# Packing attention's 74-row tail products by row copies, and holding GpSimd's residual addition

## The reference

```
x = x + relu(softmax(where(adj > 0, leaky_relu(h@a1 + (h@a2).T), -9e15)) @ h)   with h = layernorm(x) @ W
x = x + moe(layernorm(x))
```

## Time and profile before

| what | value |
|---|---|
| median of three runs | 265.56 us (265.4 to 267.12) |
| the profiled execution | 263.48 us |
| its span, first to last instruction | 261.7 us |
| TensorE busy | 250.5 us (96%) |
| VectorE, ScalarE, GpSimd busy | 180.9, 128.6, 90.1 us |
| granted TensorE clock, mean | 0.998 of full speed |

### The profile page before, as it was taken

How to read it: one execution, slowest core, us unless ns; L and a number is a source line. 1 busy time by engine, 2 the same in 40 slices (tenths; PEclk the granted TensorE clock), 3 DMA queues, 4 the chain that set the end, 5 groups by cost and what they waited for, 6 DMA issues and landing times.

```text
span 261.7 us, 4579 instructions
## 1 busy us (share of the span) xinstructions
PE 250.5 (96%) x1649; PEld 210.8 (81%) x1649; DVE 180.9 (69%) x429; ACT 128.6 (49%) x263; POOL 90.1 (34%) x113
## 2 busy tenths in 40 slices
PE   6799989999999999999999999999999999999990
PEld 1489989988888778778778889899977968879780
DVE  3988768996978977785762573847296685856931
ACT  2737786853765475555553121342447155454330
POOL 4334891000341432112120224118253834841502
PEclk9999999999999999999999999999999999999999
DMA  6990000320488888421211213136978679888001
GB/s 189 375 318 32 1 5 0 106 81 27 159 210 284 273 262 248 168 79 40 80 42 41 82 39 96 52 117 176 353 237 294 247 258 290 283 293 285 12 7 44
DMA packets 19210, 40.47 MB, mean 155 GB/s; under 512 B 2810, under 2 KB 3130, under 8 KB 19188
## 3 DMA queue, kind: packets, MB, share of 16 engines
q1 hardware_dynamic: 16196, 34.17, 39.5%
q0 software_dynamic: 2176, 4.80, 6.1%
q10 hardware_dynamic: 816, 1.21, 1.5%
HBM read 32.93 MB, written 8.31 MB: 158 GB/s over the span
## 4 chain that ended last, share of the span: by engine, by line
PE 87%; POOL 3%; DVE 2%; DMA 2%; issue 2%; ACT 2%; POOLq 1%; ACTq 0%
PE bank L1426 30%; PE bank L1690 12%; PE bank L1728 7%; PE bank L1364 6%; PE bank L1412 5%; PE bank L1756 5%; PE bank L1441 3%; PE bank L1660 2%; PE bank L1346 2%; DMA w_raw<-in_L_gnn_W_dram 2%; PE bank L1676 2%; PE bank L1703 2%; PE bank L1453 2%; PE bank L1464 2%; PE bank L1560 1%
## 5 line engine op out<-in xcount | busy, mean ns | idle before, releaser
L1426 PE MATMUL bank<-h_hi,pt_lo 128*128 128x512 f32 (+1 forms) x110 | 45.9, 417 | 0.0
L1426 PE MATMUL bank<-h_lo,pt_hi 128*128 128x512 f32 (+1 forms) x110 | 43.6, 396 | 0.0
L1426 PE MATMUL bank<-h_hi,pt_hi 128*128 128x512 f32 (+1 forms) x110 | 43.4, 394 | 0.0
L411 POOL TENSOR_TENSOR x_all<-x_all,w_raw 128x512 f32<-128x512 f32 x10 | 18.1, 1810 | 65.2 <-ACT w_raw L589 65.2
L1690 PE MATMUL bank<-prob,w 128*128 128x168 f32 x224 | 33.2, 306 | 0.0
L1690 PEld LDWEIGHTS bank<-prob,w 128*128 128x128 f32 x224 | 32.6, 189 | 0.7 <-issue 0.2
L754 ACT ACTIVATE adj_s<-bank,b_cols 128x168 f32<-128x168 f32 x28 | 11.3, 402 | 33.6 <-PE bank L1690 33.6
L1426 PEld LDWEIGHTS bank<-h_hi,pt_hi 128*128 128x128 f32 (+1 forms) x110 | 20.7, 188 | 4.9
L1426 PEld LDWEIGHTS bank<-h_hi,pt_lo 128*128 128x128 f32 (+1 forms) x110 | 20.7, 188 | 3.8
L1426 PEld LDWEIGHTS bank<-h_lo,pt_hi 128*128 128x128 f32 (+1 forms) x110 | 20.8, 189 | 3.6
L611 ACT ACTIVATE wide<-adj_s,off_b 128x1354 f32<-128x1354 f32 (+1 forms) x11 | 15.8, 1432 | 14.1 <-DVE off_b L887 14.1
(11 more groups left out here) (203 smaller groups left out, 558.1 us busy)
## 6 DMA issues: line engine op xcount, KB each, us to landing
w<-in_L_ffn_W_dram SPq DMA_DIRECT2D x16, 1024.0 KB, 6.7
adj_s<-in_adj_dram SPq DMA_DIRECT2D x10, 677.0 KB, 5.3
x_rows<-x_all SPq DMA_DIRECT2D x10, 257.0 KB, 3.2
out_dram<-x_all SPq DMA_DIRECT2D x10, 256.0 KB
...
```

What stands on the lines that cost most here:

```text
L411: pool.tensor_tensor(x_all[0:R, t, 0:D], x_all[0:R, t, 0:D], relu_s[0:R, :], ALU.add).then_inc(s_x1, 1)
L1426: ins = pe.matmul(o_ps[par][0:R, :], p[0:K, par, k, 0:R], h[0:K, k, :], start=(k == 0 and n == 0), stop=(k == NT - 1 and n == 2))
```

## The change

The last 74 columns of each row tile of probabilities are split as 64 (A) and 10 (B). The exponential of the 10 is written twice more behind the row, so that the last transposed tile has 94 rows: A, B, B, B. Three products A and three products B are then made by two: one of 128 rows with (low A, high A) against (high h of A, low h of A), and one of 94 rows with (high A, low B, high B, high B) against (high A, high B, low B, high B) of h. To have h in that order the last tile's transposed x is written with the same copies (`x_high`, `x_low` in two pieces), so that h(10) has 94 rows; ScalarE writes high h of A to `h_lo` too, VectorE writes low h of A to its lower half, and replaces the middle copy in `h_hi` by the low part with the help of a 0/1 column `is_lo`, which GpSimd makes in `low_rows`. Per row tile there are a second, short exponential, another copy in `p_high` and a third piece in `p_low`. GpSimd's `residual(t)` for t < 9 waits in addition until `p_low(t + 1)` of batch 2 is done, which in VectorE's order stands just ahead of the argument. Some small tiles of the last stage move into a tile that is free by then; this adds no instruction.

```diff
@@ -43,6 +43,10 @@
     TAIL = N - (NT - 1) * P
     CAP = N // E - 1
     S = (P, CAP - P)
+    TA = P // 2
+    TB = TAIL - TA
+    TD = TA + 3 * TB
+    NP = N + 2 * TB
     ROW = D + 2
     NOWHERE = 5000
     BATCH = ((0, 8), (8, NT - 1), (NT - 1, NT))
...
@@ -81,7 +85,7 @@
         adj_s = sb("adj_s", [P, 3, N], I32)
         wide = sb("wide", [P, 2, N])
         score2, f2b = wide[:, 0, :], wide[:, 1, :]
-        prob = sb("prob", [P, 2, N])
+        prob = sb("prob", [P, 2, NP])
         pt_hi = sb("pt_hi", [P, 2, NT, P], F32R)
         pt_lo = sb("pt_lo", [P, 2, NT, P], F32R)
         w12 = sb("w12", [P, 4, KC, D])
...
@@ -134,6 +139,7 @@
         pos = sb("pos", [P, NT])
 
         relu_s = w_raw[:, 0, 0:D]
+        h_pick = w_raw[:, 2, 0:D]
         xn2 = (w_raw[:, 2, 0:D], w_raw[:, 3, 0:D], adj_s[:, 0, 0:D].bitcast(F32))
         xg0 = adj_s[:, 2, 0:2 * D].bitcast(F32).rearrange("p (j n) -> p j n", j=2)
         b_rows = w_raw[0:E * KC, 1, 0:2 * P].rearrange("q (j p) -> q j p", j=2)
...
@@ -159,14 +165,12 @@
                                                                     ].rearrange("p (c n) -> p c n", c=KC)
                            for i in range(2)] for v in (h_hi, h_lo))
         b2_b = [prob[:, i, KC * CAP:KC * CAP + D] for i in range(2)] + [adj_s[:, 1, KC * CAP:KC * CAP + D].bitcast(F32)]
-        gate_s = sb("gate_s", [P, 2, E])
+        gate_s, emp = first[:, 0:2, :], first[:, 2:4, :]
+        dest, src = first[:, 4:6, :].bitcast(U32), first[:, 6:8, :].bitcast(U32)
         scale_s = sb("scale_s", [P, 2, 2])
         src0 = sb("src0", [P, 2], U32)
         sums = below[:, 0:6, :].rearrange("p t e -> p (t e)").rearrange("p (j e k) -> p j e k", j=2, k=3)
         gate0 = sb("gate0", [P, 2])
-        emp = sb("emp", [P, 2, E])
-        dest = sb("dest", [P, 2, E], U32)
-        src = sb("src", [P, 2, E], U32)
 
         banks = [ctx.enter_context(nc.psum_tensor(f"bank{i}", [P, 512], F32)) for i in range(8)]
         xt_ps = (banks[0], banks[1])
...
@@ -396,8 +399,22 @@
                 after(pool, s_f2, n, 2)
                 pool.tensor_tensor(dot[0:R, n % 2, :], xn[0:R, t, :], wa2_b[0:R, :], ALU.mult).then_inc(s_dot, 1)
 
+            def low_rows():
+
+
+                pool.memset(is_lo[:, 0:1], 1.0).then_inc(s_const, 1)
+                pool.wait_ge(s_const, 11)
+                pool.affine_select(out=is_lo[:, 0:1], in_=is_lo[:, 0:1], compare_op=ALU.is_ge, fill=0.0,
+                                   base=-(TA + TB), pattern=[[0, 1]], channel_multiplier=1).then_inc(s_const, 1)
+                pool.wait_ge(s_const, 12)
+                pool.affine_select(out=is_lo[:, 0:1], in_=is_lo[:, 0:1], compare_op=ALU.is_ge, fill=0.0,
+                                   base=TA + 2 * TB - 1, pattern=[[0, 1]], channel_multiplier=-1).then_inc(s_const, 1)
+                pool.wait_ge(s_const, 13)
+                pool.tensor_scalar(is_lo[:, 1:2], is_lo[:, 0:1], -2.0, 1.0, ALU.mult, ALU.add).then_inc(s_const, 1)
+
             for t in range(NT - 2):
                 power(t)
+            low_rows()
             f2_product(FCOL)
             f2_product(FCOL + 1)
             for t in range(NT - 2, NT):
...
@@ -408,6 +425,8 @@
             def residual(t):
                 R = rows(t)
                 pool.wait_ge(s_relu, t + 1)
+                if t < NT - 2:
+                    pool.wait_ge(s_plo[2], t + 2)
                 pool.tensor_tensor(x_all[0:R, t, 0:D], x_all[0:R, t, 0:D], relu_s[0:R, :], ALU.add).then_inc(s_x1, 1)
 
             def power2(t):
...
@@ -496,12 +515,20 @@
                 else:
                     if t >= 4:
                         act.wait_ge(s_h, t - 1)
-                    act.activation(xt_hi[:, par, :, 0:R], src_[:, :, 0:R], ACT.Copy).then_inc(s_xhi, 1)
+                    if t == NT - 1:
+                        act.activation(xt_hi[:, par, :, 0:TA], src_[:, :, 0:TA], ACT.Copy)
+                        act.activation(xt_hi[:, par, :, TA:TD].rearrange("p c (r n) -> p c r n", r=3),
+                                       src_[:, :, TA:TAIL].unsqueeze(2).broadcast_to([P, KC, 3, TB]), ACT.Copy
+                                       ).then_inc(s_xhi, 1)
+                    else:
+                        act.activation(xt_hi[:, par, :, 0:R], src_[:, :, 0:R], ACT.Copy).then_inc(s_xhi, 1)
 
             def h_high(t):
-                R, par = rows(t), t % 2
+                R, par = (rows(t) if t < NT - 1 else TD), t % 2
                 act.wait_ge(s_h, t + 1)
                 for j in range(2):
+                    if t == NT - 1:
+                        act.activation(h_lo[0:TA, t, j * H0:(j + 1) * H0], h_ps[par][j][0:TA, 0:H0], ACT.Copy)
                     ins = act.activation(h_hi[0:R, t, j * H0:(j + 1) * H0], h_ps[par][j][0:R, 0:H0], ACT.Copy)
                 ins.then_inc(s_hhi, 1)
 
...
@@ -600,7 +627,8 @@
                     act.activation(pt_hi[:, par, k0:k1, 0:R], v[:, :, 0:R], ACT.Copy).then_inc(s_phi[b], 1)
                 else:
                     act.activation(pt_hi[:, par, k0:k1 - 1, 0:R], v[:, 0:k1 - k0 - 1, 0:R], ACT.Copy)
-                    act.activation(pt_hi[0:TAIL, par, k1 - 1, 0:R], v[0:TAIL, k1 - k0 - 1, 0:R], ACT.Copy
+                    act.activation(pt_hi[0:TD, par, k1 - 1, 0:R], v[0:TD, k1 - k0 - 1, 0:R], ACT.Copy)
+                    act.activation(pt_lo[TA:P, par, k1 - 1, 0:R], v[0:TA, k1 - k0 - 1, 0:R], ACT.Copy
                                    ).then_inc(s_phi[b], 1)
 
             def low_slope(t):
...
@@ -617,7 +645,9 @@
 
                 after(act, s_pt[2], t, 2)
                 after(act, s_rinv, t, 2)
-                act.activation(prob[0:R, par, :], arg[t % 3][0:R, :], ACT.Exp,
+                act.activation(prob[0:R, par, N:NP].rearrange("p (r n) -> p r n", r=2),
+                               arg[t % 3][0:R, N - TB:N].unsqueeze(1).broadcast_to([R, 2, TB]), ACT.Exp)
+                act.activation(prob[0:R, par, 0:N], arg[t % 3][0:R, :], ACT.Exp,
                                accum_out=rsum[0:R, par, :]).then_inc(s_prob, 1)
 
             def x2_copy(t, par):
...
@@ -797,15 +827,36 @@
                 if t >= 4:
                     dve.wait_ge(s_h, t - 1)
                 v = xt_ps[par][:, :].rearrange("p (c n) -> p c n", c=KC)
+                if t == NT - 1:
+                    dve.tensor_tensor(xt_lo[:, par, :, 0:TA], v[:, :, 0:TA], xt_hi[:, par, :, 0:TA].bitcast(F32),
+                                      ALU.subtract)
+                    dve.tensor_tensor(xt_lo[:, par, :, TA:TD].rearrange("p c (r n) -> p c r n", r=3),
+                                      v[:, :, TA:TAIL].unsqueeze(2).broadcast_to([P, KC, 3, TB]),
+                                      xt_hi[:, par, :, TA:TD].rearrange("p c (r n) -> p c r n", r=3).bitcast(F32),
+                                      ALU.subtract).then_inc(s_xlo, 1)
+                    return
                 dve.tensor_tensor(xt_lo[:, par, :, 0:R], v[:, :, 0:R], xt_hi[:, par, :, 0:R].bitcast(F32),
                                   ALU.subtract).then_inc(s_xlo, 1)
 
             def h_low(t):
                 R, par = rows(t), t % 2
                 dve.wait_ge(s_hhi, t + 1)
+                if t == NT - 1:
+                    dve.wait_ge(s_const, 14)
                 for j in range(2):
-                    dve.tensor_tensor(h_lo[0:R, t, j * H0:(j + 1) * H0], h_ps[par][j][0:R, 0:H0],
-                                      h_hi[0:R, t, j * H0:(j + 1) * H0].bitcast(F32), ALU.subtract)
+                    c = slice(j * H0, (j + 1) * H0)
+                    if t == NT - 1:
+
+                        dve.tensor_tensor(h_lo[TA:P, t, c], h_ps[par][j][0:TA, 0:H0], h_hi[0:TA, t, c].bitcast(F32),
+                                          ALU.subtract)
+                        dve.tensor_scalar(h_pick[TA:TD, c], h_ps[par][j][TA:TD, 0:H0], is_lo[TA:TD, 0:1], None, ALU.mult
+                                          ).then_inc(s_step, 1)
+                        dve.wait_ge(s_step, j + 1)
+                        dve.scalar_tensor_tensor(h_hi[TA:TD, t, c], h_hi[TA:TD, t, c].bitcast(F32), is_lo[TA:TD, 1:2],
+                                                 h_pick[TA:TD, c], ALU.mult, ALU.add)
+                    else:
+                        dve.tensor_tensor(h_lo[0:R, t, c], h_ps[par][j][0:R, 0:H0], h_hi[0:R, t, c].bitcast(F32),
+                                          ALU.subtract)
                 k = 2 if t < FCOL else 1
                 dve.tensor_copy(f12[0:R, t, 0:k], h_ps[par][1][0:R, H0:H0 + k]).then_inc(s_hlo, 1)
 
...
@@ -911,8 +962,10 @@
                 else:
                     dve.tensor_tensor(pt_lo[:, par, k0:k1 - 1, 0:R], v[:, 0:k1 - k0 - 1, 0:R],
                                       pt_hi[:, par, k0:k1 - 1, 0:R].bitcast(F32), ALU.subtract)
-                    dve.tensor_tensor(pt_lo[0:TAIL, par, k1 - 1, 0:R], v[0:TAIL, k1 - k0 - 1, 0:R],
-                                      pt_hi[0:TAIL, par, k1 - 1, 0:R].bitcast(F32), ALU.subtract
```

(17 more changed lines are left out.)

17 lines of the change are left out of this document (8 added, 9 removed).

## The result

The changed kernel takes **269.24 us** (median of 4 runs, 267.41 to 270.1), the kernel before beside it 265.48 us (4 runs, 263.67 to 267.12). The ratio is 1.0144, 95% interval 1.0095 to 1.0192: slower by 1.4%. Forecast were 265.1 us and a range that ended at 266.7, so the prediction was wrong, in sign and in range.

A forecast was written before the change was run, and what follows sets the result against it. TensorE was taken to bound the kernel, its matmuls busy for 96% of the span. Terms -2.55 + 1.0 + 0.9 + 0.2 = -0.45 us took 265.56 to 265.1 us, range 263.5 to 266.7.

The forecast's parts named there:

- What is added in the opening of attention: Start of attention: VectorE's added work on tile 10 makes TensorE wait at tile 1, +0.9 us.
- The rule I had cited: VectorE: an instruction starting in another quadrant of 32 partitions waits for all earlier ones; would hold the pieces at partition 64.
- My third rival: VectorE's new pieces in p_low(0) and h_low(10) each held, 0.56 us together: +0.1, 265.7 us; chance 0.14.
- So TensorE stays the bound, and 0.58 us a tile are left: Later tiles: VectorE's and ScalarE's loop takes 9.2 us against TensorE's 9.78, so their added work costs nothing.
- At the end of attention: Before the dispatch: ScalarE's extra copy delays the exponential leading to places(0), returning +0.2 us.
- the price of `low_rows`: GpSimd before attention, between power(8) and f2_product(6): added instructions delay TensorE by their whole length, +1.0 us.
- the removed product: TensorE, each row tile: two products for three save 0.232 us in ten tiles, 0.23 in the last; -2.55 us.
- the packed product at the old pace: TensorE, each row tile: the product of 94 rows for 74 keeps its pace; extra cost taken as zero.
- the sixth rival: TensorE: packed product slower than the pace, costing what the removed one did; 267.7 us, chance 0.03.
- the fourth: GpSimd: the two selects cost 0.63 us, low_rows 1.9 us in place of 1.0; +0.45, 266.0 us, chance 0.12.
- The hold: GpSimd's residual: extra wait for the last low part moves it 0.1 to 0.4 us in early tiles; costs nothing.
- The fifth rival: Later tiles: the residual addition beside VectorE's argument slows VectorE, which becomes the bound; +0.9, 266.5 us, chance 0.04.

The follow-up runs named there:

- experiment 6: Changed kernel without the product and the sum that put the low part into the middle copy of h in h_low(10): 266.46 us, ratio 1.0038.
- experiments 11: Kernel before plus an unused third ten-row piece at partition 0 in p_low's last batch, for all tiles but two: 264.37 us, one run.
- experiment 12: Kernel before plus an unused third ten-row piece at partition 64 in p_low's last batch, for all tiles but two: 265.31 us, one run.
- Experiment 10: Changed kernel with low_rows first on GpSimd, one-step pick, VectorE's p_low(1) and argument(2) earlier, exp_below(0) earlier, relu_out still ahead of x2_copy: 263.17 us, ratio 0.9912.
- Experiment 8: Changed kernel with low_rows first on GpSimd, one-step pick, VectorE's p_low(1) and argument(2) earlier, ScalarE's x2_copy and exp_below(0) earlier: 262.99 us, ratio 0.9929.
- experiment 2: Changed kernel with low_rows moved to the head of GpSimd's queue: 267.68 us, ratio 1.0149.

## Why the prediction was wrong

**"What is added in the opening of attention" (+0.9 us): this term failed.** VectorE's lateness was to be 1.95 us. Its first low part of tile 1 began at 68.18 us, without idle time, where 60.69 was the earliest before, and 4.55 us are the later `f2_turn`: 2.94 us. `h_low(10)` grew by 3.06 - 0.73 = 2.33 in place of 1.6, `p_low(0)` by 0.41 in place of 0.2, `x_low(10)` by 0.2. TensorE reached the second batch of tile 1 at 73.70 us, 6.75 later than the 66.95 of before. The later `f2_turn` less one saved product explains 4.55 - 0.23 = 4.32 of that; the rest is a stall of 2.4 us, 1.5 over the forecast (experiment 6 takes 2.2 of it away). I priced the new instructions at the pitch of neighbours that all begin at partition 0. Theirs is that of instructions that start only when the one ahead has ended: 0.43 to 0.52 us against 0.33 in `h_low(10)`, 0.31 against 0.19 in experiment 12. The start partition alone is told apart for one piece in the late batch (experiments 11 and 12); for the six instructions of `h_low(10)` it rests on the traces, where the subtractions overlap in experiment 6 and do not with a pick or a sum between them. The rule I had cited speaks of this (the Trainium skill, VectorE: DVE Perf Modes, section Two Vector instructions with no wait between them), and this trace agrees. My third rival had the mechanism, but priced it at 0.56 us for seven instructions and added only 0.1 to the end; the picks and sums also last longer, 0.47 to 0.48, than the 0.42 of the plain subtraction.

**"So TensorE stays the bound, and 0.58 us a tile are left" (nothing forecast): this step failed too, +1.4 us.** It was right for turns 4 to 9 (9.80 us) and wrong for turn 3. Two things were off. The size: the loop grew by 0.71 us a tile, not by 0.15 + 0.20, since VectorE's piece costs 0.41 and ScalarE's copy delays the low part by 0.27 (why ScalarE's copies follow at 0.28 us in place of 0.15, no run tells). And the question: I compared the two rates, and not how far ahead the slower loop was at the first reader of its work. In the first turns TensorE gains 0.23 us each, VectorE and ScalarE lose 0.7, and `x2_copy`, last in ScalarE's row, had 0.93 us in hand. That this is not the opening's lateness is shown by experiment 6, where the wait stays at 1.23. Turn 3 takes 11.15 to 11.20 us in every packed kernel that keeps the argument at 1.63 us, whatever the opening and the order; no experiment removes this loss, so that `x2_copy` is its cause is argued from the trace. Experiment 10 against 8 shows that it is more than the order of the two copies.

**At the end of attention: 0.2 forecast, 0.63 us measured**, by the same kind of chain, `places(0)` behind `exp_below(0)` behind ScalarE's added work. Experiment 8, which puts `exp_below(0)` a step ahead, has no wait there; it changes VectorE's order and ScalarE's copies as well, so how much of the 0.63 that one edit takes is not told apart.

**Right:** the price of `low_rows`, 0.85 us for 1.0, nearly all of it passed on to TensorE (0.8, experiment 2); the removed product (period 9.80 for 9.78, so 0.22 of 0.23 us a turn), though the last tile's 0.23 us were not seen; the packed product at the old pace (the sixth rival falls); GpSimd's selects at 0.19 us (the fourth falls).

**The hold: nothing forecast, nothing lost, but for another reason.** The wait moves the addition by 0.38 us (relu out at 93.30, addition at 93.68), as estimated, though in seven of ten tiles and not in the early ones alone, and what counts is on which side of the argument's start that puts it. I had read "the argument's 1.62 us are the same with it and without" (the addition), and that holds only if the argument starts first or nearly so. The fifth rival (VectorE slowed by the addition, over 9.78 us a tile) is what happens without the hold: the hold keeps off 3.1 us that the changed kernel would lose besides. Hence the terms, forecast and measured: removed products -2.55 and -2.2, `low_rows` +1.0 and +0.8, opening +0.9 and +2.4, later turns 0 and +1.4, end +0.2 and +0.6; together -0.45 and +3.0.

What stays open: some 0.6 us between the 3.0 of the traces and the 3.6 to 3.8 of the runs. The runs of before at a clock of 0.993 or more spread from 263.0 to 265.1 us, and the changed kernel has one such run, so it can't be placed.
